# Four-layer cross-attention on one core: the second gram wave of a step moved from behind the second scores to behind the turned maxima, and its weighing ahead of the residual addition

## The reference, cut to what matters

```
q = heads(x @ W_q);  k_t = heads(text @ W_k);  v_t = heads(text @ W_v)
probs_t = softmax(q k_t * attn_scale);  text_out = probs_t v_t
qsem = einsum('bhst,bte->bhse', probs_t, text)
qsem = qsem / max(norm(qsem), EPS);  ip_n = ip / max(norm(ip), EPS)
fused = q k_ip * attn_scale + 0.5 * (qsem . ip_n)
probs_ip = softmax(fused) * spatial_mask
x = (text_out + probs_ip v_ip) @ W_out + b_out + x
```

## Time and profile before

| | |
|---|---|
| median of 3 runs | 2298.52 us (2294.76 to 2299.3) |
| the profiled execution | 2298.45 us, its span 2296.7 us |
| PE busy | 2091.2 us (91%) |
| PEld busy | 1698.9 us (74%) |
| DVE busy | 1485.5 us (65%) |
| ACT busy | 1084.5 us (47%) |
| POOL busy | 459.7 us (20%) |
| mean granted TensorE clock | 0.967 |

### The profile page before, as it was taken

The page is one execution under the profiler, slowest core; times in us unless marked ns, Lnnn a source line. Parts: engine busy times, 40 slices in busy tenths (PEclk is TensorE's granted clock), DMA queues, the critical chain, the costliest instruction groups (busy, mean ns, idle before and its releaser), DMA issues.

```text
span 2296.7 us, 75803 instructions
## 1 busy us (share of the span) xinstructions
PE 2091.2 (91%) x26394; PEld 1698.9 (74%) x26394; DVE 1485.5 (65%) x4449; ACT 1084.5 (47%) x2733; POOL 459.7 (20%) x870
## 2 busy tenths in 40 slices
PE   1789999999999999999999999999999999999975
PEld 1567777777777777778777777777777787777764
DVE  3236676676677667667766766776676677667653
ACT  0245454455445445544554554454455455555431
POOL 0112221212112121211222122121212112121210
PEclk9789999999999999999999999999999999999985
DMA  3111111111111121111111111111211111111000
GB/s 81 51 39 50 51 45 39 51 44 42 47 51 44 40 51 44 39 51 51 43 42 51 44 42 48 51 44 40 51 44 40 50 51 44 39 51 37 24 10 5
DMA packets 108575, 101.30 MB, mean 44 GB/s; under 512 B 42240, under 2 KB 84952, under 8 KB 108184
## 3 DMA queue, kind: packets, MB, share of 16 engines
q1 hardware_dynamic: 104556, 92.88, 15.0%
q10 hardware_dynamic: 3628, 3.33, 0.5%
HBM read 34.13 MB, written 5.41 MB: 17 GB/s over the span
## 4 chain that ended last, share of the span: by engine, by line
PE 76%; DVE 12%; issue 6%; SPq 2%; ACT 1%; DMA 1%; ACTq 1%; DVEq 0%; POOLq 0%; POOL 0%
PE ps_s L736 12%; PE ps_c L814 9%; PE ps_s L769 9%; PE ps_k L642 7%; PE ps_c L881 6%; PE ps_k L834 5%; DVE top L1120 5%; PE ps_s L786 4%; PE ps_q L715 4%; PE ps_c L870 4%; PE ps_k L839 4%; PE ps_c L886 3%; DVE weighted L1160 3%; PE ps_k L679 2%; PE ps_c L847 2%
## 5 line engine op out<-in xcount | busy, mean ns | idle before, releaser
L1120 DVE TENSOR_REDUCE top<-ps_s 128x6 f32<-128x462 f32 (+3 forms) x1024 | 514.1, 546 | 199.1 <-PE ps_s L736 194.0
L1018 ACT ACTIVATE p_t<-ps_s 116x512 f32<-116x512 f32 (+1 forms) x768 | 371.8, 545 | 67.2 <-PE ps_s L769 67.0
L736 PE MATMUL ps_s<-k_blocks,q_sb 32*128 32x231 f32 (+1 forms) x3584 | 334.3, 384 | 18.3 <-issue 18.1
L1160 DVE TENSOR_TENSOR weighted<-ps_k,probs 128x462 f32<-128x462 f32 (+1 forms) x256 | 143.2, 559 | 249.3 <-PE ps_k L839 247.1
L814 PE MATMUL ps_c<-p_t,v_rows 116*27 116x128 f32 (+1 forms) x7168 | 283.1, 280 | 13.6 <-DMA v_rows<-v_img 11.1
L1341 POOL TENSOR_TENSOR k_blocks<-k_sb,mask_k 128x231 f32<-128x231 f32 x384 | 212.5, 576 | 374.1 <-PE ps_s L769 358.1
L736 PEld LDWEIGHTS ps_s<-k_blocks,q_sb 32*128 32x128 f32 x3584 | 220.7, 186 | 74.8 <-issue 46.9
L814 PEld LDWEIGHTS ps_c<-p_t,v_rows 116*27 116x27 f32 (+1 forms) x7168 | 210.5, 107 | 83.5 <-issue 48.4
L769 PE MATMUL ps_s<-q_sb,k_blocks 32*116 32x128 f32 (+1 forms) x5376 | 229.1, 287 | 37.6 <-DVE probs L1135 23.8
L642 PE MATMUL ps_k<-context,wk 128*128 128x154 f32 (+1 forms) x1024 | 170.5, 309 | 98.5 <-DVE weighted L1160 58.6
L769 PEld LDWEIGHTS ps_s<-q_sb,k_blocks 32*116 32x116 f32 (+1 forms) x5376 | 191.8, 179 | 74.2 <-issue 58.8
(11 more groups left out here) (118 smaller groups left out, 3573.0 us busy)
## 6 DMA issues: line engine op xcount, KB each, us to landing
v_rows<-v_img SPq DMA_DIRECT2D x128, 227.4 KB
context<-in_ctx SPq DMA_DIRECT2D x64, 336.0 KB, 3.1
q_sb<-top_t SPq DMA_DIRECT2D x576, 6.0 KB
v_rows<-v_img SPq DMA_DIRECT2D x64, 115.2 KB
v_rows<-v_img SPq DMA_DIRECT2D x64, 112.2 KB
v_rep<-v_dram SPq DMA_DIRECT2D x64, 50.0 KB
q_sb<-top_t SPq DMA_DIRECT2D x192, 2.0 KB
gram<-g_img SPq DMA_DIRECT2D x64, 46.3 KB
```

Source lines behind the costliest of these rows:

```text
L736: ins = pe.matmul(ps_s[:, z * 512 + j * GT:z * 512 + j * GT + n], q_sb[c % 3][lo:lo + QUAD, j * S:(j + 1) * S], k_blocks[c % 3][lo:lo + QU ...
L1018: act.activation(to, source, ACT.Exp, scale=SCALE).then_inc(p_ready, 1)
L1120: dve.tensor_reduce(top[c % 2][:, z * BH:z * BH + m], s.rearrange("p (h t) -> p h t", t=T)[:, :, 0:n], AX.X, ALU.max).then_inc(s_top, 1)
L1160: dve.tensor_tensor(weighted[:, lo * T:hi * T], ps_k[:, 0:(hi - lo) * T], probs[:, lo * T:hi * T], ALU.mult).then_inc(w_ready, 1)
```

## The change

The second wave of a time moves on TensorE from behind `second` to ahead of it, right behind `turn_top`. The weighing of that wave moves on VectorE from behind `new_x` to ahead of it. No instruction is added or taken away.

```diff
@@ TensorE, step @@
                 if topped(t):
                     turn_top(k, t)
+                if e_waves(t):
+                    gram_wave(k, t, 1)
                 if exists(t - 1):
                     second(k, t - 1)
-                if e_waves(t):
-                    gram_wave(k, t, 1)
                 if exists(t - 2):
                     turn_back(k, t - 2)
@@ VectorE, step @@
                 if ip(t - 6):
                     image_branch(k, t - 6, 16, 19)
+                if e_waves(t):
+                    weigh(k, t, 1)
                 if out(t):
                     new_x(k, t)
-                if e_waves(t):
-                    weigh(k, t, 1)
                 if ip(t - 6):
                     image_branch(k, t - 6, 19, 21)
```

## The result

The changed kernel takes 2348.18 us (median of 4 runs, 2345.87 to 2356.35), the kernel before 2298.7 us in the same runs: a ratio of 1.0225, 95% interval 1.0198 to 1.0253. It is slower by 49 us. The prediction was 2355, its range 2328 to 2372. The profiled execution took 2345.87 us, its span is 2344.1 against 2296.7, 47.4 us more.

The account below looks back on a forecast made before the run. TensorE was taken to bound the kernel, with 76% of the chain that ended last. Losses of 0.40 and 0.49 us over 63 pairs of times, 56 us on 2298.45, gave 2355 us, range 2328 to 2372.

Parts of the forecast that it names:

- The keys' wait goes: On TensorE, the keys (L642) no longer wait for the second weighing: 0.59 us saved at time 1, 0.53 at time 2.
- The second wave waits for the first weighing: On TensorE at L834, both waves use `ps_k`: new wait of 0.69 us at time 1, 0.78 at time 2.
- The exponentials' tie: ScalarE's last exponential holds the next scores' banks: times 1 and 2 longer by 0.40 and 0.49 us; chance 0.79.
- The witness for it: Sign in the profile after: L736 waits for `p_t` L1018 more than 150 times, not 46.
- Matmuls alone: Rival: ScalarE frees its banks in time, so TensorE's 0.20 and 0.35 us alone count; 2333 us, chance 0.12.
- My 0.10 for the wave ahead of the scores: On TensorE, the second wave was estimated to last up to 0.10 us longer ahead of the second scores.
- VectorE's move costs nothing: On VectorE, the weighing ahead of the residual addition costs nothing, as the addition waits for the projection's end.
- VectorE would come too late at time 1: Rival: VectorE's 0.4 us cover gone, another 0.3 lost each time 1; 2374 us, within the 0.79 for exponentials in force.
- POOL does nothing else or earlier: POOL and the DMA queues were said to issue nothing else or earlier.
- The clock: Rival: longer waits lower TensorE's granted clock in wave times, say 1 us a time; 2480 us, chance 0.03.
- The sum: Whole kernel: 0.40 + 0.49 = 0.89 us a pair of times, 63 pairs, 56 us slower.

Follow-up runs that it names:

- two kernels that touch ScalarE alone: On the changed kernel: f_exp put ahead of the four bank exponentials, 2346.27 us; or the last bank's exponential halved at times 1 and 2, 2328.5 us.
- the half that was only there to serve the other: Against the kernel before, only the weighing moved ahead of the residual addition on VectorE, TensorE's order kept: 2288.33 us, ratio 0.996.
- the best mixture: Changed kernel with f_exp first; time 1 also has its first wave ahead of the output projection, time 2 has TensorE's old order: 2272.13 us, ratio 0.9886.
- the run with f_exp first: Changed kernel with f_exp (L1035) ahead of a time's four bank exponentials instead of between the second and third: 2346.27 us, ratio 1.0197.

## Why the prediction was right, step by step

*The keys' wait goes.* Right: from 120 waits to one.

*The second wave waits for the first weighing, 0.69 and 0.78.* Right: 128 waits, 0.68 each in the mean, 0.72 in the row of time 2. Announced were 85 to 95 us, measured 87.5.

*The exponentials' tie takes over.* Right in place and size, and shown by two kernels that touch ScalarE alone: 0.40 and 0.49 announced, 0.38 and 0.48 measured in the mean. The distance of 0.43 from the last exponential to the queries' tail, read at time 3, held at both new places. There is some luck in the 0.40: it was read off one time 1, and the typical one loses 0.48 (9.61 to 10.09) while the mean loses 0.38.

*The witness for it.* Wrong: I announced that L736 would wait for L1018 more than 150 times. The trace after lists, as what ended the idle time of the engine at L736:

```profile
  ACT p_t L1018: 15.8, 77
```

77 instead of 46. The first banks' matmuls run while the last bank is awaited, and where they cover the wait the profile sees no idle engine. The distance from L736 to L708 (0.39, 0.66, 0.82) shows the tie; the list of waits shows only part of it.

*Matmuls alone, 0.20 and 0.35.* Mis-sized, and without weight only because the tie lies above. In the rows after, the tie takes 0.43 of time 1 and 0.27 of time 2, so matmuls alone would be at -0.05 and +0.21. Medians say the same more plainly: counted from the first L814 of a time, the next scores start at 7.12 both before and after at time 1, and at 6.39 before and 6.62 after at time 2, so 0.00 and +0.23; the tail of the queries moves from 7.51 to 7.98 and from 6.77 to 7.28. One reason shows in the rows: keys that don't wait need 1.14 to the next scores, while I kept the 1.19 and 1.25 of keys that do. My 0.10 for the wave ahead of the scores was right (0.61 against 0.51).

*VectorE's move costs nothing.* Right in the whole change. That VectorE would come too late at time 1 did not happen: time 1 grew by 0.38, not 0.70, and from the tail of the queries to the next L814 it takes 2.11 before and after (medians). VectorE and ScalarE are busy for 1500.4 and 1078.4 us against 1485.5 and 1084.5, the same to 1%. But "at nothing" was an understatement for time 2: made alone, the same move gains 0.26 a time 2.

*POOL does nothing else or earlier.* It does nothing else, but it works later, since it waits for the second scores (L769) before it writes `k_blocks`. The weight loads of L736 now wait for it (L1341) 27 times, 4.4 us in all, where they did not before. All 27 are at times 1. They cost nothing yet: from the keys to the next scores pass 1.14 in the time 1 above, which has this wait, and 1.14 in the time 2, which does not.

*The clock.* The rival was a lowered clock in the wave times. The window of a time 2 after, with its wait of 0.62 to 0.72 in it, PEclk third from the end:

```profile
1240.00:1249.00 9.00, 8.38 (x116) 7.22 (x115) 3.86 (x11) 4.12 (x10) 3.27 (x5) 1.00 0.23 61
```

It stays at 1.00, and so it does through the whole loop but for stretches behind its edges (below). The Trainium skill, "TensorE: Matmul & The Clock Gate", section "A second HAM failure mode: psum-queue depth-cycling", has short idle stretches make the clock oscillate; waits of 0.7 us twice a period did not do so here.

*The sum.* 63 x 0.89 = 56 us against 49. Times 1 and 2 give 63 x 0.86 = 54. Behind the 49 stand two terms that the forecast did not have, and that it came so close is in part luck. By the starts of L814 the profiled run is 1.5 us longer up to time 16, with two pairs of wave times in it; 36.1 us longer from there to time 236, where 55 pairs give 47 and 11 come back at the loop's edges; and 9.7 us longer from there to the end (226.1 to 235.8), where seven pairs would give 6. So the edges took 11 off and the end added some 4. Without either the time would have been some 7 us longer, still within the range. The windows of that end, before and after:

```profile
2070.60:2296.70 226.10, 180.78 (x1961) 148.09 (x1960) 134.05 (x419) 82.15 (x203) 35.72 (x66) 0.83 0.07 19
```

```profile
2108.20:2344.10 235.90, 187.56 (x1962) 153.01 (x1960) 135.55 (x420) 81.48 (x203) 35.73 (x66) 0.82 0.07 18
```

The granted clock is 0.83 before and 0.82 after, so part of the 9.7 is time at the lower level. How much of it the change brought about is not shown.

## What to carry to other kernels

Moving work ahead of a producer does two things: it may wait for what it used to be spaced from, and it no longer covers what the producer's consumer does afterwards. Look for the second as well: here ScalarE had 1.49 and 0.94 us to spare, the move used 1.85 and 1.39, and neighbouring stages already showed what the tie looks like with nothing to spare. When a change bundles several moves, try each alone and each at each stage: the half that was only there to serve the other was a gain of 0.4% by itself, and the best mixture 1.1%.

## What the runs showed of the hardware that was not expected

The granted clock behind the loop's eight edges differs from profile to profile. At each edge TensorE stands still for some 2 us (1.86 to 2.52 before, 1.86 to 2.49 after). Windows of 6 us behind the edges, before (four of eight, the others at 0.72, 0.72, 0.72 and 0.50), then after (four of eight, the others at 1.00):

```profile
1001.00:1007.00 6.00, 5.97 (x61) 4.75 (x62) 4.14 (x14) 1.15 (x3) 0.00 (x0) 0.72 0.02 7
1202.10:1208.10 6.00, 6.00 (x75) 5.30 (x76) 3.89 (x13) 2.37 (x7) 0.00 (x0) 1.00 0.03 7
1402.20:1408.20 6.00, 5.97 (x63) 5.17 (x64) 4.07 (x14) 1.15 (x3) 0.00 (x0) 0.72 0.03 7
1804.30:1810.30 6.00, 6.00 (x61) 5.04 (x62) 4.14 (x14) 1.15 (x3) 0.00 (x0) 0.72 0.02 7
```

```profile
401.40:407.40 6.00, 5.98 (x61) 5.08 (x62) 3.70 (x12) 1.15 (x3) 0.00 (x0) 0.72 0.03 6
607.60:613.60 6.00, 5.99 (x76) 5.31 (x76) 3.92 (x13) 2.36 (x7) 0.00 (x0) 1.00 0.02 6
1221.50:1227.50 6.00, 5.93 (x75) 5.25 (x76) 3.84 (x13) 2.30 (x7) 0.00 (x0) 1.00 0.03 7
1836.00:1842.00 6.00, 5.96 (x75) 5.28 (x76) 4.34 (x15) 2.33 (x7) 0.00 (x0) 1.00 0.03 8
```

Part of seven of these windows ran at 1.2 GHz before, of one after: a window at 0.72 holds some 61 matmuls, one at 1.00 some 75. In the table it shows at the edges' times, 3 and 0, which together are shorter by 0.25 us a period. Some 0.25 x 40 = 10 us thus came back over the middle of the kernel, and in the run with f_exp first, with five such edges, some of it went again. It is the edges alone: a typical time 3 takes 6.69 and a typical time 0 6.68 (medians) in each of the eleven kernels. The mean of times 3 and 0 together follows the number of edges with a lowered clock behind them: 13.83 with one, 13.91 with two, 13.96 to 13.99 with four or five, 14.05 to 14.17 with six or seven.

Why the clock falls at one edge and not at another, the runs don't settle. The length of the stop does not tell: before, it fell behind a stop of 1.86 us and not behind one of 1.97; after, behind one of 1.87 and not behind one of 2.49. Nor is it shown that the kernel decides it, since there is one profile of each, and the mean granted clock differs as much between runs of one kernel: 0.967 to 0.974 after, 0.965 to 0.973 before. It is enough to hide a gain of 10 us in one profile: differences of that size are better read from the stages than from the total.
